# Decoder block with 32 experts on one core: the shared expert's gate and up products of later sequences at the end of the first stage, and later turns in an order written out

## The chip, the cores and the metric

The kernel runs on one core of one Trainium2 chip. The metric is the device time of one execution in microseconds (us), the median of three runs. PE is TensorE, DVE VectorE, ACT ScalarE, POOL GpSimd; SP only issues DMAs here.

## The reference

One post-norm decoder layer in float32 over 16 sequences of 256 tokens, width 256:

```
q, k, v = x Wq' + bq, x Wk' + bk, x Wv' + bv                # one head of 256
theta   = 0.5 + 0.2 sigmoid(qk) + 0.15 tanh(qk) + 0.1 relu(qk)
x1      = layernorm(x + softmax(theta) v Wo' + bo)
x2      = layernorm(x1 + cross attention(x1, ctx))          # 16 heads of 16, chunks of 64 tokens
scores  = sigmoid(x2 Wr')                                   # 32 experts in 4 groups
topk    = the 4 best experts out of the 2 best groups, weights normed to 2.5
mixed   = sum over the 4 of w * down_e( silu(gate_e x2) * up_e x2 )    # 128 inner
shared  = down_s( silu(gate_s x2) * up_s x2 )                          # 256 inner
out     = layernorm(x2 + mixed + shared)
```

## The kernel before

There are three stages. The first runs attention, cross attention, the router and the inner half of the shared expert, one sequence at a time in a software pipeline; each token's row is scattered to the region of each of its experts in `routed`. The second takes 159 blocks of 128 routed rows through their experts. The third adds the parts and normalizes.

The first stage is the subject. Every engine has its own instruction stream, in program order; semaphores join them. The order is written as a loop over turns `t` with one branch per step: turn `t` runs the first attention of sequence `t`, the cross attention of `t-2` and the router of `t-4`. After turn 15 the same loop runs six turns more, in which ever fewer steps are live; this text calls them the drain. A turn is counted from `pe_scores2(t-2)`, PE's scores of the cross attention (L398).

The steps that matter below:

- `pe_gate(i)` (L488) and `pe_up(i)` (L497): the shared expert's gate and up products, eight matmul records each, into PSUM banks 6 and 7. In the loop `pe_gate(t-4)` and `pe_up(t-5)` are in every turn. ACT makes tanh of the gate (`act_gates`, L841), DVE the two products (`vec_hs1`, L1065, and `vec_hs2`, L1070), and SP stores the result (`store_hs`, L1317) to `inner`, from where it is read in the second stage. `hs` has two buffers, so `act_gates(i)` waits for the store of `i-2`.
- `pe_scores1` (L338), then tanh on ACT (L761, L762), four instructions on DVE up to the row maximum `nmx` (`vec_th`, L943 to L949), exp on ACT (L768), and `pe_prT(t)` (L283 out of `pr_tile`): the softmax of the first attention leaves PE and comes back to it.
- `pool_xc` (L1239) and `pool_xc2` (L1256): residual sums on POOL, two instructions each. `pool_scattera` and `pool_scatterb` (L1263, L1269): four indirect DMAs each, 128 rows each.
- `pe_tables` (L512 to L522) with `vec_tables` (to L1120): the block tables, made once the last rank is known. SP's row loads of the second stage (L1370) wait for `v_adr` (L1119) and for every scatter.
- `load_rest` (L1328): the experts' weights, 768 KB for each sequence. The share of the first 14 comes during the turns. The room of the last two (`LATE = 2`) serves as work space in the first stage, so they are loaded only after the last `pe_scores2`.

## Time and profile before

| | us |
|---|---|
| median of three runs | 829.56 |
| the three runs | 825.52, 829.56, 829.70 |
| the profiled execution | 825.1 |
| its span, first to last instruction | 823.3 |
| PE busy, share of the span | 759.4, 92% |
| DVE busy | 581.7, 71% |
| ACT busy | 494.2, 60% |
| POOL busy | 367.9, 45% |

Busy time is what an engine's instructions took; matmul records overlap a little, so eight that the timeline lists with 1.89 us follow one another in 1.73 us, and the chain of waits shows the second number. A time below is in us from the span's start, if not said otherwise. What lies around the span is 1.8 us (825.1 less 823.3).

### The profile page before, as it was taken

What the parts mean: (1) busy time and instruction counts of PE and PEld (TensorE: products, weight loads), DVE (VectorE), ACT (ScalarE), POOL (GpSimd) and SP (SyncE); (2) the same over time, 40 slices, a digit from 0 to 9 for tenths busy, and PEclk for the clock granted to TensorE, in tenths of its full rate; (3) what the DMA queues carried; (4) which work ended last, traced back from release to release, by engine and by line L of the source; (5) the groups of instructions that cost most, each with busy time, mean ns of one, the idle gap of its engine ahead of it and who ended that gap; (6) DMA issues with size and microseconds to landing.
All of it is one profiled execution on the core that took longest, in us unless ns stands there. A gap on an engine that the chain in (4) does not pass through costs nothing.

```text
span 823.3 us, 21802 instructions
## 1 busy us (share of the span) xinstructions
PE 759.4 (92%) x8308; PEld 660.5 (80%) x8308; DVE 581.7 (71%) x2093; ACT 494.2 (60%) x1166; POOL 367.9 (45%) x437
## 2 busy tenths in 40 slices
PE   7969899999999999999987656799999999999996
PEld 6758788888888888888876536799999999998554
DVE  2345487898889888898898863466666666665585
ACT  0546666767777767767664414566666766663133
POOL 0110214335543455335545762466666666665142
PEclk9999999999999999999999977999999999999998
DMA  6572221332343334332113436755555555552996
GB/s 235 163 210 84 85 85 53 105 123 93 132 134 104 110 117 130 106 121 94 65 60 111 143 116 186 290 168 176 177 164 179 168 169 170 179 161 91 376 400 238
DMA packets 69642, 124.95 MB, mean 152 GB/s; under 512 B 9665, under 2 KB 43329, under 8 KB 69282
## 3 DMA queue, kind: packets, MB, share of 16 engines
q1 hardware_dynamic: 51394, 81.60, 31.4%
q0 software_dynamic: 13776, 37.77, 12.7%
q10 hardware_dynamic: 4368, 4.20, 1.5%
q8 instruction: 66, 1.08, 0.5%
q14 instruction: 38, 0.31, 0.1%
HBM read 73.16 MB, written 50.36 MB: 150 GB/s over the span
## 4 chain that ended last, share of the span: by engine, by line
PE 78%; DMA 7%; DVE 6%; SPq 5%; issue 2%; POOL 1%; ACT 1%; ACTq 0%; DVEq 0%
PE banks L537 17%; PE banks L283 10%; PE banks L544 8%; PE banks L385 4%; PE banks L376 3%; PE banks L353 3%; PE banks L321 3%; PE banks L366 3%; SPq L566 3%; PE banks L488 3%; PE banks L330 3%; PE banks L462 3%; PE banks L497 3%; PE banks L338 3%; DMA w_expert_tile<-y 2%; PE banks L428 2%
## 5 line engine op out<-in xcount | busy, mean ns | idle before, releaser
L1291 POOL DMA_INDIRECT y<-yb_tile,idcol_tile x159 | 152.4, 959 | 110.3 <-DVE yb_tile L1143 106.9
L537 PE MATMUL banks<-xbT_tile,wgu_tile 128*128 128x128 f32 x1272 | 170.4, 278 | 0.0
L537 PEld LDWEIGHTS banks<-xbT_tile,wgu_tile 128*128 128x128 f32 x1272 | 157.2, 195 | 0.1
L1143 DVE SCALAR_TENSOR_TENSOR yb_tile<-banks,rowsb_tile 128x256 f32<-128x256 f32 x159 | 76.9, 483 | 81.3 <-PE banks L544 73.1
L856 ACT ACTIVATE wgu_tile<-w_expert_tile 128x512 f32 x159 | 98.9, 622 | 11.8 <-DVE tab_i_tile L1120 11.8
L544 PE MATMUL banks<-w_expert_tile,hb_tile 128*128 x318 | 95.9, 384 | 4.8 <-DVE hb_tile L1131 4.8
L1269 POOL DMA_INDIRECT routed<-row_tile,idx_tile x64 | 62.5, 977 | 65.9 <-PE banks L398 50.4
L852 ACT ACTIVATE gb_tile<-banks 128x128 f32<-128x128 f32 x159 | 44.1, 277 | 77.5 <-PE banks L537 77.4
L1263 POOL DMA_INDIRECT routed<-row_tile,idx_tile x64 | 61.7, 963 | 30.7 <-issue 18.5
L1244 POOL TENSOR_TENSOR rs_tile<-ve_tile,half_neg_tile 128x2 f32<-128x2 f32 x16 | 11.1, 693 | 143.5 <-DVE ve_tile L959 143.5
L283 PE MATMUL banks<-const_tile,rowsb_tile 128*128 128x128 f32 x318 | 61.9, 277 | 7.1 <-DMA rowsb_tile<-routed 7.1
L723 ACT ACTIVATE xbT_tile<-banks 128x256 f32<-128x256 f32 x159 | 59.8, 376 | 12.2 <-PE banks L283 12.0
L283 PEld LDWEIGHTS banks<-const_tile,rowsb_tile 128*128 128x128 f32 x318 | 45.1, 143 | 23.5 <-DMA rowsb_tile<-routed 7.9
L544 PEld LDWEIGHTS banks<-w_expert_tile,hb_tile 128*128 128x128 f32 x318 | 48.5, 193 | 5.9 <-issue 5.9
L1131 DVE TENSOR_TENSOR hb_tile<-hb_tile,banks 128x128 f32<-128x128 f32 x159 | 45.8, 288 | 5.5
L1128 DVE SCALAR_TENSOR_TENSOR hb_tile<-gb_tile,banks 128x128 f32<-128x128 f32 x159 | 44.7, 281 | 3.9 <-ACT gb_tile L852 3.9
L1239 POOL TENSOR_TENSOR xc_tile<-x_sb_tile,c_out_tile 128x256 f32<-128x256 f32 x32 | 22.7, 734 | 54.7 <-ACT x_tile L815 27.7
L637 ACT ACTIVATE w_expert_tile<-w_expert_tile,fnmr_tile,frs_tile 128x256 f32<-128x256 f32 x32 | 17.6, 593 | 48.6 <-DVE fnmr_tile L617 48.6
L630 POOL TENSOR_TENSOR frs_tile<-fve_tile,fhalf_tile 128x2 f32<-128x2 f32 (+1 forms) x17 | 18.0, 1056 | 42.7 <-DVE fve_tile L612 42.7
L321 PE MATMUL banks<-xT_tile,g_qk_tile 128*128 128x256 f32 x128 | 32.4, 398 | 3.6 <-DMA xT_tile<-xT 3.6
L497 PE MATMUL banks<-x2T_tile,w_shared_in_tile 128*128 128x256 f32 x128 | 32.5, 400 | 1.3 <-ACT sc_tile L835 1.3
L594 PE MATMUL banks<-w_expert_tile,const_tile 128*128 128x512 f32 (+1 forms) x68 | 30.4, 580 | 3.5 <-DMA w_expert_tile<-y 3.5
(205 smaller groups left out, 1778.3 us busy)
## 6 DMA issues: line engine op xcount, KB each, us to landing
rowsb_tile<-routed SPq DMA_DIRECT2D x159, 129.0 KB, 2.2
w_expert_tile<-y SPq DMA_DIRECT2D x15, 1024.0 KB, 15.1
w_expert_tile<-w_expert SPq DMA_DIRECT2D x16, 768.0 KB
cT_tile<-ctxT SPq DMA_DIRECT2D x16, 384.0 KB, 2.9
routed<-zrow_tile SPq DMA_DIRECT2D x1, 4128.0 KB, 21.9
xT_tile<-xT SPq DMA_DIRECT2D x16, 256.0 KB, 3.1
x_sb_tile<-x SPq DMA_DIRECT2D x16, 256.0 KB, 2.8
inner<-hs_tile SPq DMA_DIRECT2D x16, 256.0 KB, 2.2
```

The lines of the kernel that those rows point to most:

```text
L283: return e.transpose(o, i, ident)
L321: m = e.matmul(bank[5][:, db * S:(db + 1) * S], g_qk[:, k, db * P:(db + 1) * P], xT[:, k, :], start=k == 0, stop=k == DK - 1)
L497: m = e.matmul(bank[7][:, b * S:(b + 1) * S], w_shared_in[:, k, 2 * P + b * P:3 * P + b * P], x2T[i % 2][:, k, :], start=k == 0, stop=k == ...
L537: m = e.matmul(bank[2 + u % 4][:, h * P:(h + 1) * P], wgu[u % WG][:, k * D + h * EI:k * D + (h + 1) * EI], xbT[u % 2][:, k * P:(k + 1) * P ...
L544: e.matmul(bank[6 + u % 2][:, 0:D], hb[u % 4][:, :], w_flat[:, bass.ds(w + 2 * D, D)], start=True, stop=True).then_inc(SEM["p_down"], 1)
L723: e.activation(o, i, ACT.Copy).then_inc(SEM[done], 1)
L856: e.activation(wgu[u % WG][:, :], w_flat[:, bass.ds(w, DK * D)], ACT.Copy)
L1131: e.tensor_tensor(hb[u % 4][:, :], hb1[u % 2][:, :], bank[2 + u % 4][:, EI:2 * EI], ALU.mult)\
L1143: e.scalar_tensor_tensor(yb[n % YS][:, :], bank[6 + u % 2][:, 0:D], rowsb[n % ROWS][:, D:D + 1], rowsb[n % ROWS][:, 0:D], ALU.mult, ALU.ad ...
L1263: e.indirect_dma_start(routed, bass.IndirectOffsetOnAxis(ap=idx[i % 2][:, 0, k:k + 1], axis=0), row[i % 2][:, k, 0, :], None).then_inc(SEM ...
L1269: e.indirect_dma_start(routed, bass.IndirectOffsetOnAxis(ap=idx[i % 2][:, 1, k:k + 1], axis=0), row[i % 2][:, k, 1, :], None).then_inc(SEM ...
L1291: e.indirect_dma_start(y, bass.IndirectOffsetOnAxis(ap=idcol[n % ROWS][:, :], axis=0), yb[n % YS][:, :], None).then_inc(SEM[f"st_y{n % YS} ...
```

## The change

Turns 0 to 7 stay in the loop. From the ninth on (turn 8) each engine has its own written list of steps, and the waits that belonged to the loop (`looped`) are written between the steps. Gate and up of sequences 4 to 15 are no longer in "their" turns: `pe_up(3)` is in turn 11, gate and up of 4 in turn 14, and the rest from turn 15 on. For this `x2T` has ten buffers instead of two. The room comes from the experts' weights: `qT`, `kM`, `vM`, `sha`, `shb` and both `prT` lie in it now, and `LATE` is 6, so the last six shares are loaded after the last `pe_av2`.

```diff
-        LATE = 3072 // SHARE
+        LATE = 9216 // SHARE
...
-        x2T = [sa(f"x2T{u}", [P, DK, S]) for u in range(2)]
+        x2T = [sa(f"x2T{u}", [P, DK, S]) for u in range(10)]
...
-        def pe_gate(e, i):
-            after(e, SEM["a_vo"], min(i + 5, nseq))
-            after(e, SEM["v_ve2"], min(i + 2, nseq))
+        def pe_gate(e, i, looped=True):
+            if looped:
+                after(e, SEM["a_vo"], min(i + 5, nseq))
...
-            for t in range(nseq + 6):
+            for t in range(8):
...
+            pe_out2(e, 14)
+            pe_x2T(e, 13, False)
+            e.wait_ge(SEM["v_ve2"], 15)
+            pe_gate(e, 7, False)
+            e.wait_ge(SEM["a_x2T"], 14)
+            pe_router(e, 13)
...
+            e.wait_ge(SEM["v_ve2"], 16)
+            pe_gate(e, 8, False)
+            e.wait_ge(SEM["a_sc"], 15)
+            pe_up(e, 8, False)
+            e.wait_ge(SEM["a_hg"], 9)
+            e.wait_ge(SEM["v_h1"], 9)
+            pe_gate(e, 9, False)
+            e.wait_ge(SEM["v_hs"], 9)
+            pe_up(e, 9, False)
...
         def act_gates(e, i):
             e.wait_ge(SEM["p_sg"], i + 1)
-            after(e, SEM["st_hs"], 16 * (i - 1))
+            after(e, SEM[f"st_hs{i % 2}"], 16 * (i // 2))
...
+            act_row(e, 14)
+            act_gates(e, 9)
+            act_norm2(e, 15)
+            act_x2T(e, 15)
...
+            vec_x2(e, 15, ch)
+            vec_route(e, 14, ch)
+            vec_hs1(e, 8, ch)
+            vec_hs2(e, 8, ch)
+            vec_choice(e, 14, ch)
+            vec_hs1(e, 9, ch)
+            vec_hs2(e, 9, ch)
+            vec_key(e, 14, ch)
+            vec_route(e, 15, ch)
...
                 if i == nseq - LATE:
                     e.wait_ge(SEM["p_s2"], nseq)
+                    e.wait_ge(SEM["p_av2"], nseq)
...
-                if live(t - 6):
+                if 0 <= t - 6 <= 2:
                     store_hs(e, t - 6)
+                if 3 <= t - 11 <= 3:
+                    store_hs(e, t - 11)
                 if 0 < t <= nseq - LATE:
                     load_rest(e, t - 1)
-                if nseq < t <= nseq + LATE:
-                    load_rest(e, t - 1 - LATE)
+            for i in range(4, 7):
+                store_hs(e, i)
+            for i in range(nseq - LATE, nseq):
+                load_rest(e, i)
+            for i in range(7, 16):
+                store_hs(e, i)
```

Three places show what moved. The first is PE in the middle of a turn, from the scores of the first attention to the transposes of its softmax. L338 (L341 after) is `pe_scores1`, L497 up, L488 gate, L376 (L382) `pe_v`, L366 (L371) `pe_k`; the L283 (L284) rows are transposes, those out of `pr_tile` being `pe_prT`. Before, in every turn:

```order
L338 MATMUL banks<-xT_tile,zT_tile 128x256 x4
L497 MATMUL banks<-x2T_tile,w_shared_in_tile 128x256 x4
L283 MATMUL banks<-const_tile,sha_tile 128x128 x8
L488 MATMUL banks<-x2T_tile,w_shared_in_tile 128x256 x4
L376 MATMUL banks<-w_cross_tile,cT_tile 128x128 x8
L283 MATMUL banks<-const_tile,x_tile 128x128 x4
L283 MATMUL banks<-const_tile,shb_tile 128x128 x8
L366 MATMUL banks<-cT_tile,w_cross_tile 128x256 x4
L283 MATMUL banks<-const_tile,pr_tile 128x128 x4
```

After, in turn 10 (L488 is the router there):

```order
L341 MATMUL banks<-xT_tile,zT_tile 128x256 x4
L488 MATMUL banks<-w_router_tile,x2T_tile 128x32 x4
L284 MATMUL banks<-const_tile,w_expert_tile 128x128 x8
L284 MATMUL banks<-const_tile,x_tile 128x128 x4
L382 MATMUL banks<-w_cross_tile,cT_tile 128x128 x8
L284 MATMUL banks<-const_tile,w_expert_tile 128x128 x8
L284 MATMUL banks<-const_tile,pr_tile 128x128 x4
L371 MATMUL banks<-cT_tile,w_cross_tile 128x256 x4
```

Gate and up are gone from between them, the router has come in from before `pe_scores1`, and `pe_k` stands behind `pe_prT`.

The second is PE's end of the first stage: the last products before the tables (L512 before, L520 after); L504 and L505 (L513, L514) are `pe_rank`, L479 (L488 after) the router. Before:

```order
L462 MATMUL banks<-w_cross_tile,num_tile 128x256 x4
L283 MATMUL banks<-const_tile,x_tile 128x128 x4
L479 MATMUL banks<-w_router_tile,x2T_tile 128x32 x4
L497 MATMUL banks<-x2T_tile,w_shared_in_tile 128x256 x4
L488 MATMUL banks<-x2T_tile,w_shared_in_tile 128x256 x4
...
L504 MATMUL banks<-msel_tile,const_tile 128x64
L505 MATMUL banks<-macc_tile,const_tile 128x64
L497 MATMUL banks<-x2T_tile,w_shared_in_tile 128x256 x4
L512 MATMUL banks<-const_tile,macc_tile 32x1
```

After (L497 is gate, L506 up), from the last router on:

```order
L488 MATMUL banks<-w_router_tile,x2T_tile 128x32 x4
L497 MATMUL banks<-x2T_tile,w_shared_in_tile 128x256 x4
L506 MATMUL banks<-x2T_tile,w_shared_in_tile 128x256 x4
L497 MATMUL banks<-x2T_tile,w_shared_in_tile 128x256 x4
L506 MATMUL banks<-x2T_tile,w_shared_in_tile 128x256 x4
L513 MATMUL banks<-msel_tile,const_tile 128x64
L514 MATMUL banks<-macc_tile,const_tile 128x64
L497 MATMUL banks<-x2T_tile,w_shared_in_tile 128x256 x4
L506 MATMUL banks<-x2T_tile,w_shared_in_tile 128x256 x4
L497 MATMUL banks<-x2T_tile,w_shared_in_tile 128x256 x4
L506 MATMUL banks<-x2T_tile,w_shared_in_tile 128x256 x8
L497 MATMUL banks<-x2T_tile,w_shared_in_tile 128x256 x8
```

Six pairs of gate and up (10 to 15) stand behind the last router, where one pair and one up stood, and two pairs (8 and 9) stand just before it.

The third is POOL in one turn, from its scatters on. L1239 (L1977 after) is `pool_xc`, L1256 (L1995) `pool_xc2`, L1250 (L1988) the power of the second norm. Before:

```order
L1269 DMA routed<-row_tile,idx_tile 135168x258 x4
L1263 DMA routed<-row_tile,idx_tile 135168x258 x4
L1239 TENSOR_TENSOR xc_tile<-x_sb_tile,c_out_tile 128x256 x2
L1256 TENSOR_TENSOR xc_tile<-x_tile,c_out_tile 128x256 x2
L1250 TENSOR_TENSOR rs_tile<-ve_tile,half_neg_tile 128x2
```

After, in turn 9:

```order
L2009 DMA routed<-row_tile,idx_tile 135168x258 x4
L2002 DMA routed<-row_tile,idx_tile 135168x258 x4
L1988 TENSOR_TENSOR rs_tile<-ve_tile,half_neg_tile 128x2
L1990 TENSOR_TENSOR nmr_tile<-neg_tile,rs_tile 128x2
L1977 TENSOR_TENSOR xc_tile<-x_sb_tile,c_out_tile 128x256 x2
L1995 TENSOR_TENSOR xc_tile<-x_tile,c_out_tile 128x256 x2
```

The power comes ahead of the sums in turns 8, 9, 11 and 13; in turns 10 and 12 `pool_xc` follows the scatters directly, as before.

## Rows read from the trace of the kernel before

**Rows 1.** Busy time in stretches: turns 8 to 15, the drain in two parts (columns: PE, PEld, DVE, ACT, POOL; clock)
```profile
208.00:420.40 212.40, 211.90 (x3074) 187.17 (x3072) 186.00 (x641) 151.89 (x330) 98.57 (x128) 1.00 0.32 108
420.40:459.50 39.10, 30.61 (x638) 25.64 (x638) 33.53 (x124) 20.67 (x32) 23.99 (x28) 1.00 0.28 98
459.50:498.20 38.70, 20.01 (x85) 14.72 (x83) 25.05 (x128) 8.04 (x11) 24.06 (x26) 0.78 0.37 129
```

**Rows 2.** Chain of waits in turn 13 (start, us, what)
```profile
340.75 1.14 PE banks L398 x63
...
344.20 0.81 PE banks L479 x8
...
348.56 1.73 PE banks L497 x8
...
357.71 0.43 PE banks L283 x4
```

**Rows 3.** Timeline of turn 13: the softmax outside PE, and POOL (start, us, engine)
```profile
342.18 1.04 POOL L1269 DMA_INDIRECT routed<-row_tile,idx_tile  x1 [4.35 <-PE banks L398]
...
348.60 0.47 ACT L761 ACTIVATE w_expert_tile<-banks,r_half_tile 128x256 f32<-128x256 f32 x1 [0.26 <-PE banks L338]
...
352.09 1.42 POOL L1239 TENSOR_TENSOR xc_tile<-x_sb_tile,c_out_tile 128x256 f32<-128x256 f32 x2
...
352.58 2.31 DVE L949 TENSOR_SCALAR nmx_tile<-mx_tile 128x2 f32<-128x2 f32 x1
...
353.46 1.40 POOL L1256 TENSOR_TENSOR xc_tile<-x_tile,c_out_tile 128x256 f32<-128x256 f32 x2
...
354.93 0.51 ACT L768 ACTIVATE pr_tile<-w_expert_tile,nmx_tile 128x256 f32<-128x256 f32 x1 [1.77 <-DVE nmx_tile L949]
```

**Rows 4.** Timeline: PE's first work of turns 8, 14, 16 and of the tables; DVE's addresses
```profile
208.16 1.21 PE L398 MATMUL banks<-kM_tile,qT_tile 32*64 32x128 f32 x64
...
367.19 1.21 PE L398 MATMUL banks<-kM_tile,qT_tile 32*64 32x128 f32 x64
...
420.41 1.21 PE L398 MATMUL banks<-kM_tile,qT_tile 32*64 32x128 f32 x64
...
486.22 0.20 PE L512 MATMUL banks<-const_tile,macc_tile 128*32 128x1 f32 x2 [1.34 <-DVE hs_tile L1070]
...
492.12 0.24 DVE L1119 TENSOR_SCALAR tab_i_tile<-tab_tile 1x160 int32<-1x160 f32 x1
```

**Rows 5.** Chain of waits at the end of the first stage
```profile
479.19 0.61 ACT hs_tile L841
...
494.63 2.56 DMA routed<-row_tile,idx_tile
497.28 0.72 SPq L269
498.21 0.36 SPq L1370
```

**Rows 6.** Busy time in three stretches: DVE from route to choice, its key and x2, one weight share
```profile
354.81:360.95 6.14, 6.14 (x95) 5.23 (x93) 5.52 (x39) 5.37 (x9) 0.96 (x3) 1.00 0.33 108
365.51:369.92 4.41, 4.41 (x82) 3.63 (x82) 4.10 (x18) 3.13 (x12) 1.04 (x1) 1.00 0.72 242
120.00:122.00 2.00, 2.00 (x68) 1.59 (x69) 1.07 (x4) 0.68 (x1) 0.00 (x0) 1.00 1.01 415
```

**Rows 7.** The page's DMA issues: count, KB each, median us to landing
```profile
routed<-zrow_tile SPq DMA_DIRECT2D x1, 4128.0 KB, 21.9
...
hs_sb_tile<-inner SPq DMA_DIRECT2D x1, 4096.0 KB, 14.5
```

**Rows 8.** Timeline of SP: the load of xT for turn 2
```profile
41.68 0.96 SPq L1301 DMA_DIRECT2D xT_tile<-xT  x1
```

**Rows 9.** Landing of a line's 16 DMAs: L1301 (loads of xT), then L1317 (stores of hs)
```profile
DMA to landing us min/median/max: 2.5/3.1/12.7
...
DMA to landing us min/median/max: 2.0/2.2/4.1
```

More of the change, by code:

```diff
@@ new lines, in _ @@
+            e.wait_ge(SEM["v_mxb"], 7)
+            e.wait_ge(SEM["v_shb"], 7)
+            pe_pTa(e, 6, False)
+            pe_x1T(e, 7)
+            e.wait_ge(SEM["a_vo"], 9)
+            pe_v(e, 8, False)
+            e.wait_ge(SEM["a_pTa"], 7)
+            pe_pTb(e, 6)
+            e.wait_ge(SEM["v_mx"], 9)
+            pe_prT(e, 8)
+            pe_k(e, 8)
+            e.wait_ge(SEM["a_pTb"], 7)
+            pe_av1(e, 8)
+            pe_den(e, 6)
+            pe_av2(e, 6, False)
+            pe_rank(e, 4)
@@ new lines, in _ @@
+            pe_scores1(e, 9)
+            e.wait_ge(SEM["a_x2T"], 6)
+            pe_router(e, 5)
+            e.wait_ge(SEM["v_mxa"], 8)
+            e.wait_ge(SEM["v_mxb"], 8)
+            e.wait_ge(SEM["v_shb"], 8)
+            pe_pTa(e, 7, False)
+            e.wait_ge(SEM["a_vo"], 10)
+            pe_v(e, 9, False)
+            pe_x1T(e, 8)
+            e.wait_ge(SEM["a_pTa"], 8)
+            pe_pTb(e, 7)
+            e.wait_ge(SEM["v_mx"], 10)
+            pe_prT(e, 9)
+            pe_k(e, 9)
@@ new lines, in _ @@
+            e.wait_ge(SEM["v_mxb"], 10)
+            e.wait_ge(SEM["v_shb"], 10)
+            pe_pTa(e, 9, False)
+            e.wait_ge(SEM["a_vo"], 12)
+            pe_v(e, 11, False)
+            pe_x1T(e, 10)
+            e.wait_ge(SEM["a_pTa"], 10)
+            pe_pTb(e, 9)
+            pe_k(e, 11)
+            e.wait_ge(SEM["v_hs"], 4)
+            pe_x2T(e, 8, False)
+            pe_prT(e, 11)
+            e.wait_ge(SEM["a_pTb"], 10)
+            pe_den(e, 9)
+            pe_av1(e, 11)
+            pe_av2(e, 9, False)
@@ new lines, in _ @@
+            pe_vo(e, 12, False)
+            e.wait_ge(SEM["a_z"], 13)
+            pe_scores1(e, 12)
+            pe_router(e, 8)
+            e.wait_ge(SEM["v_mxa"], 11)
+            e.wait_ge(SEM["v_mxb"], 11)
+            e.wait_ge(SEM["v_shb"], 11)
+            pe_pTa(e, 10, False)
+            pe_x1T(e, 11)
+            e.wait_ge(SEM["a_vo"], 13)
+            pe_v(e, 12, False)
+            e.wait_ge(SEM["a_pTa"], 11)
+            pe_pTb(e, 10)
+            e.wait_ge(SEM["v_mx"], 13)
+            pe_prT(e, 12)
@@ new lines, in _ @@
+            pe_scores1(e, 14)
+            e.wait_ge(SEM["a_vo"], 15)
+            pe_v(e, 14, False)
+            pe_gate(e, 4, False)
+            e.wait_ge(SEM["v_sha"], 13)
+            pe_pTa(e, 12, False)
+            pe_up(e, 4, False)
+            e.wait_ge(SEM["a_pTa"], 13)
+            pe_pTb(e, 12)
+            e.wait_ge(SEM["v_mx"], 15)
+            pe_prT(e, 14)
+            pe_k(e, 14)
+            e.wait_ge(SEM["a_pTb"], 13)
+            pe_den(e, 12)
+            pe_av1(e, 14)
+            e.wait_ge(SEM["v_h1"], 5)
@@ L860, in _ @@
             e.wait_ge(SEM["v_setup"], 1)
-            for t in range(nseq + 6):
+            for t in range(8):
                 if live(t - 4):
@@ L1275, in _ @@
             e.wait_ge(SEM["v_setup"], 3)
-            for t in range(nseq + 6):
+            for t in range(8):
                 if live(t - 6):
```

797 lines of the change are left out of this document (748 added, 49 removed).

## The prediction

> **What bounds the kernel now.** I read the page's slices first: PE is nine tenths busy nearly everywhere, with one dip in the middle, at the end of the first stage. Busy time in stretches gives it numbers [rows 1]: in turns 8 to 15 PE is busy 211.9 of 212.4 us, so PE sets the pace there and every PE instruction costs its full time. In the first half of the drain it is busy 30.6 of 39.1 us, in the second 20.0 of 38.7, and there the granted clock is 0.78: part of it ran at 1.2 GHz instead of 2.4, after gaps of PE. So 27 us of PE lie idle in the drain, while gate and up, which nothing needs before the second stage, stand in the full turns. Then the chain of waits: in a turn it is all PE [rows 2]; at the end of the first stage it runs from the last sequence's router over DVE to POOL's eight scatters, whose last lands at 497.2, and SP starts the row loads 0.93 us later, at 498.2 [rows 5]. The addresses for them are ready at 492.4 [rows 4], so the tables are not what ends the stage; the scatters are.
>
> **The turns (8 to 13).** Six turns take (367.19 - 208.16) / 6 = 26.51 us each [rows 4]. Gate and up are 1.73 us each [rows 2], so PE's own work in a turn falls to 26.51 - 3.46 = 23.05. Whether the turn gets there is decided by what the two products covered: the way of the softmax out of PE and back. In before, PE leaves `pe_scores1` at 348.56 and starts `pe_prT` at 357.71, 9.15 us later, all filled [rows 2]. In after, router, `pe_pTa`, `pe_x1T`, `pe_v` and `pe_pTb` stand between: 9.15 less gate and up (3.46) less `pe_k` (1.73, eight records of the same size as up) plus the router's 0.81, 4.8 us. The way itself: tanh starts at 348.60 and `nmx` at 352.58, 3.98 [rows 3]; `nmx` alone is some 0.2 when nothing stops it; two exps of 0.51 and handing over 1.1; with hops 5.4. So the turn becomes one chain: PE from `pe_scores2` to the end of `pe_scores1` without the router, 348.56 - 340.75 - 0.81 = 7.0; the softmax 5.4; and from `pe_prT` to the next turn 367.19 - 357.71 = 9.48, plus `pe_k` 1.73, 11.2. That is 23.6; I add 0.2, since DVE now waits once for `pe_vo`: 23.8. On DVE the turn is 186.0 / 8 = 23.3 busy [rows 1], less 1.2 for the two products that go with gate and up, 22.1 at most: close behind, not ahead.
>
> `nmx` is the weak place. It took 2.31 us and ended at 354.89, just as POOL's four sums did (353.46 + 1.40 = 354.86) [rows 3]: a tiny DVE instruction held up while POOL adds in SBUF. In before that was hidden by the 9.15. In after, `nmx` starts 7.0 + 4.0 = 11.0 us into the turn, and POOL's sums could start 352.09 - 340.75 = 11.3 us in, where they follow the scatters directly (turns 10 and 12), and 1.0 later where the power stands ahead. So it slips through by 0.3 us in two turns and by 1.3 in four. I price turns 10 and 12 at 2.0 together (bounds: nothing, and 2 x 2.8). Turn 11 carries `pe_up(3)`, 1.73, of which a little fills a gap: 1.4. Sum 6 x 23.8 + 2.0 + 1.4 = 146.2 against 159.0: -12.8. Bounds: at PE's own work -19.0, at the old turn length 0.
>
> **Turns 14 and 15.** Turn 14 has gate and up as before: 26.6. Turn 15 has gate but no up, and `pe_v(15)` and `pe_out2(13)` (1.78 each, as eight such records) go over to turn 16: 26.5 - 1.7 - 3.6 = 21.2 of PE, with waits 22.6. Together 49.2 against 420.41 - 367.19 = 53.2: -4.0.
>
> **The drain.** Up to `pe_out2(15)` before takes 39.1 [rows 1]. After, I walked through the written lists step by step with the durations of the trace: turn 16 holds 18.9 us of PE and takes 20, turn 17 holds 14.8, but waits for DVE's four passes over banks 0 to 3 and takes 20: 40.0 in all, +0.9. The fillers (up 5, gate and up 6, gate and up 7) are free there.
>
> Behind it stand eight pairs of gate and up, 27.7 us, and 3.7 of transposes, routers and ranks: 31.4 of PE. DVE has route and choice twice (6.14 less one product, 5.5 each), key and x2 4.4, key twice more 5.0, and sixteen products of 0.6: 30 [rows 6]. Two engines with 31 and 30 that hand each other every bank do not overlap fully. Step by step from the end of `pe_out2(15)`: gate 8 waits for x2 (2.7), gate 9 for the product of 8, which stands behind route 14 (7.2), gate 10 at 13.4, gate 11 behind route 15 (18.4), gate 13 behind key 15 (25.9), then 3.6 us per pair (gate 1.73, ACT 0.61 [rows 5], product 0.6, hops), the last up ends at 38.5, the tables start at 39.4. Before, it was 486.22 - 459.5 = 26.7: +12.7. Bounds: 31.4 without a wait, +4.7; PE with the two routes and the last key laid bare, 31.4 + 11 + 2.5, +18.2. I take the walk, near their middle.
>
> **The store behind the weights.** SP now issues six weight shares (4.72 MB) after the last `pe_av2`, and `store_hs(7)` behind them; `act_gates(9)` waits for that store, and gate 10 and the second norm of 15 for ACT. A store lands in 2.2 us as a rule [rows 9]. But the load issued at 41.68 [rows 8] came behind the 4128 KB that landed in 21.9 us [rows 7], and is the one of 12.7 among 16 loads with a median of 3.1 [rows 9]. At the rate of a weight share, 415 GB/s [rows 6], the six take 11.4 us; at that of the `hs_sb` load, 4096 KB in 14.5 us [rows 7], 16.3. Gate 9 ends 12.6 us after `pe_av2(15)`; with 0.6 for issue and 2.2 for landing the store is 1.6 or 6.5 us late. Bounds 0 (no order between them) and 6.5; I take +2.5, near the row of the same kind of transfer. The weights themselves are in some 30 us before they are needed.
>
> The Trainium skill, "DMA: Bandwidth & Descriptors", section "Queues, rings and completion order", says that each DMA engine consumes the descriptors of one ring in ring order, SP having one ring on each. By that rule the store waits for all six shares and the term is 1.6 to 6.5; with shares moved side by side it would be 0. The load of 12.7 us above agrees with the rule.
>
> **The end of the stage.** The last key now ends 25 us after `pe_out2(15)`, the scatters are through 13 us later and landed before the tables are done. SP is released by the addresses: 492.36 + 0.93 = 493.3 in before's terms, not 498.2: -4.9. The short matmuls of the tables still leave PE idle before the second stage, so I leave its first blocks at the lower clock as they are.
>
> **Sum.** -12.8 - 4.0 + 0.9 + 12.7 + 2.5 - 4.9 = -5.6 us on the profiled execution's 825.1: 819.5. The median shown is 829.56, 4.5 above that execution (the three runs are 825.5, 829.6, 829.7); the same step from it gives 824.0. I forecast between the two: 822.
>
> **Rivals.**
> - *PE's own work is reached.* The softmax fits (5.4 against 4.8 is a close call), no stop in turns 10 and 12, and the store is free: 6 x 23.05 + 1.7 = 140.0 instead of 146.2, and 2.5 less: 810.8. For it: PE had not one gap in these turns. Against: the chain counted above.
> - *DVE takes the turn over at 25.* POOL's sums then hold up not `nmx` but a copy in `vec_route` (up to 1.4 us for one pair), and `vec_rden`, `vec_x1`, `vec_o` come late for `pe_spread` and `pe_out2`. 6 x 1.2 more: about 826 to 827, no change.
> - *Slower: `nmx` is stopped in every turn.* If it starts after POOL's first sum, it waits until POOL's pairs are over, 2.8 us, now uncovered: the turn is 23.6 + 2.8 = 26.4 again. In all six, 14.8 more than I count: 834.3. It is slower than before as soon as about four turns more than counted are stopped. For it: a margin of 0.3 us in two turns, and it happened in turn 13. Against: 1.3 us in the other four.
> - That gate and up stay where they were is excluded by the order of PE.
>
> **How the numbers follow.** A measurement here can tell about 0.5%, 4.1 us, from no change. The forecast (815 to 824 on the profiled scale) 0.46, of which 0.33 is faster by more than that; PE's own work 0.17, faster; turns of 25 us 0.22, same 0.17; stopped every turn 0.15, slower 0.13. Faster 0.53, same 0.32, slower 0.15. The range 811 to 831 goes from the first rival to the stopped turns in part; the likeliest case alone is 815 to 828, the difference between runs included.
>
> **What would show it.** `pe_scores2` to `pe_scores2` in turns 8 to 13: 23.8; a gap of PE before `pe_prT` under 1 us; `nmx` at 0.2 us, and at 1.5 or more where stopped. Turn 16 starts at 403.6, the tables at 485.5, the first row load at 492.6 with no wait for a scatter. ACT's `act_gates(9)` released by a DMA, not by PE. It is wrong if turns stay above 25, if the stage's tail is longer than 43 us from `pe_out2(15)`, or if SP still waits for scatters.

## The result, and the profile after

The changed kernel took 837.13 us (median of five runs, 833.12 to 839.35) against 827.09 for before (five runs): ratio 1.0097, interval 1.0067 to 1.0127. Forecast was 822 with a range of 811 to 831, so the sign was wrong as well as the size. The profiled execution took 835.56 us, its span 833.7. In three of the five sessions below every kernel, before included, took 4 to 5% longer (before at 860 to 871 us, elsewhere at 827 to 830), so a ratio is always to before in the same session.

The stages, from the starts of the same matmuls in the two traces (before [rows 4, 5]; "forecast" are the terms of the prediction; the last row counts from the end of `pe_out2(15)`, as the row above it does):

| stretch, us | before | forecast | after |
|---|---|---|---|
| start of turn 8 | 208.16 | 208.2 | 209.85 |
| turns 8 to 13 | 159.0 | 146.2 | 149.5 |
| turns 14, 15 | 53.2 | 49.2 | 48.8 |
| turn 16 to the end of `pe_out2(15)` | 39.1 | 40.0 | 43.0 |
| from there to the tables | 26.7 | 41.9 | 49.6 |
| from there to the first row load | 38.7 | 49.0 | 56.7 |

The misses are +3.3, -0.4, +3.0, +7.7, and +1.7 for the start, 15.3 of the 16.1 by which the execution is over the 819.5 of the sum. The start stays open: six later runs of the new order began turn 8 at 206.8 to 209.7, one of them, the unchanged kernel again, at 209.65. The same stretches as busy time (stretch; then per engine us busy and instructions; granted clock of PE, DMA share, GB/s), where [rows 1] has those of before:

```profile
209.85:359.34 149.49, 142.19 (x2217) 125.79 (x2216) 128.88 (x473) 108.36 (x235) 75.31 (x96) 0.99 0.29 97
359.34:408.10 48.76, 47.58 (x733) 41.55 (x733) 41.97 (x151) 38.23 (x83) 24.66 (x32) 1.00 0.22 70
408.10:451.10 43.00, 35.51 (x670) 31.11 (x671) 36.34 (x134) 21.06 (x35) 24.02 (x28) 1.00 0.27 94
451.10:500.70 49.60, 37.14 (x160) 30.54 (x158) 27.66 (x119) 10.99 (x16) 24.02 (x26) 0.86 0.49 187
451.10:507.80 56.70, 40.23 (x172) 31.88 (x170) 31.20 (x135) 10.99 (x16) 24.02 (x26) 0.83 0.44 168
467.00:480.00 13.00, 10.23 (x33) 8.52 (x34) 8.64 (x44) 4.67 (x7) 6.27 (x7) 0.56 0.22 80
```

First column after the length: PE. Up to the first row load it idles 7.3 + 1.2 + 7.5 + 16.5 = 32.5 us; in before it was 0.5 + 8.5 + 18.7 = 27.7 [rows 1]. The change moved PE's idle time and made it 4.8 us longer. 12.5 us of it lie between `pe_out2(15)` and the tables, and there a stretch of 13 us ran at a clock of 0.56. The waits around 467 us (start, us, engine line; in brackets idle time before, and who ended it) say why:

```profile
446.93 4.29 SPq L2133 DMA_DIRECT2D w_expert_tile<-w_expert  x6
451.26 0.44 SPq L2121 DMA_DIRECT2D inner<-hs_tile  x1
466.88 0.60 ACT L1233 ACTIVATE hs_tile<-banks 128x512 f32<-128x512 f32 x1 [9.02 <-DMA inner<-hs_tile]
467.50 0.69 DVE L1650 SCALAR_TENSOR_TENSOR hs_tile<-hs_tile,banks 128x512 f32<-128x512 f32 x1 [6.74 <-ACT hs_tile L1233]
469.04 1.11 PE L284 MATMUL banks<-const_tile,x_tile 128*128 128x128 f32 x4 [6.51 <-DVE hs_tile L1656]
470.88 1.89 PE L488 MATMUL banks<-w_router_tile,x2T_tile 128*128 128x32 f32 x8 [0.73 <-ACT x2T_tile L1111]
472.58 3.76 PE L497 MATMUL banks<-x2T_tile,w_shared_in_tile 128*128 128x256 f32 x8
476.14 3.04 PE L506 MATMUL banks<-x2T_tile,w_shared_in_tile 128*128 128x256 f32 x8
```

SP issues the six weight shares, then the store of `hs(7)`; it lands 15.5 us later. ACT's gate 9 waits for it, DVE's products for ACT, and PE's transposes of `x2(15)` for DVE. Behind the gap PE runs at 1.2 GHz: a gate takes 3.76 us where it took 1.97 to 2.00 in front. And who lets SP start the row loads:

```profile
SPq L270 <- DVE tab_i_tile L1702: 5.6, 1, 5.6
507.80 1.41 SPq L2181 DMA_DIRECT2D rowsb_tile<-routed  x3
```

The addresses, as forecast, and no scatter any more (before: [rows 5]).

### The profile page after: what moved, and what is told of

It reads as the page before. It is cut to its first block, busy times and chain, and to the rows that moved or that the text cites. A ratio compares the mean times of both kernels' runs of the same rounds, so it can differ in the third digit from the quotient of the medians.

```text
span 833.7 us, 21846 instructions
## 1 busy us (share of the span) xinstructions
PE 763.7 (92%) x8308; PEld 664.2 (80%) x8308; DVE 575.1 (69%) x2093; ACT 493.3 (59%) x1166; POOL 369.5 (44%) x437
## 4 chain that ended last, share of the span: by engine, by line
PE 75%; DMA 8%; DVE 8%; SPq 5%; issue 2%; ACT 1%; POOL 0%; ACTq 0%; DVEq 0%
PE banks L545 17%; PE banks L284 9%; PE banks L552 8%; PE banks L390 4%; PE banks L323 3%; PE banks L470 3%; PE banks L497 3%; PE banks L506 3%; PE banks L382 3%; PE banks L333 3%; PE banks L371 3%; PE banks L356 3%; SPq L574 3%; DMA w_expert_tile<-y 2%; PE banks L404 2%
## 5 line engine op out<-in xcount | busy, mean ns | idle before, releaser
L2002 POOL DMA_INDIRECT routed<-row_tile,idx_tile x64 | 62.7, 980 | 41.2 <-PE banks L404 23.0
L284 PE MATMUL banks<-const_tile,rowsb_tile 128*128 128x128 f32 x318 | 62.1, 278 | 2.1 <-DMA rowsb_tile<-routed 2.1
L284 PEld LDWEIGHTS banks<-const_tile,rowsb_tile 128*128 128x128 f32 x318 | 45.3, 143 | 18.5 <-DMA rowsb_tile<-routed 2.8
L1977 POOL TENSOR_TENSOR xc_tile<-x_sb_tile,c_out_tile 128x256 f32<-128x256 f32 x32 | 22.8, 734 | 55.8 <-ACT x_tile L1208 28.5
L284 PE MATMUL banks<-const_tile,w_expert_tile 128*128 128x128 f32 x256 | 33.6, 274 | 9.2 <-DVE w_expert_tile L1575 8.5
L284 PEld LDWEIGHTS banks<-const_tile,w_expert_tile 128*128 128x128 f32 x256 | 28.7, 141 | 12.1 <-issue 10.1
L497 PE MATMUL banks<-x2T_tile,w_shared_in_tile 128*128 128x256 f32 x128 | 32.7, 401 | 4.6 <-DVE hs_tile L1650 2.8
```

Source lines behind the costliest of these rows:

```text
L284: return e.transpose(o, i, ident)
L497: m = e.matmul(bank[6][:, b * S:(b + 1) * S], w_shared_in[:, k, 0 * P + b * P:1 * P + b * P], x2T[i % 10][:, k, :], start=k == 0, stop=k = ...
L2002: e.indirect_dma_start(routed, bass.IndirectOffsetOnAxis(ap=idx[i % 2][:, 0, k:k + 1], axis=0), row[i % 2][:, k, 0, :], None).then_inc(SEM ...
```

## The experiments

Only the sessions in which before took 827 to 830 us decide here; the runs of the others have a section of their own below. An indented paragraph is what was expected, as it was written before the run.

**1. The store first.**

```
-            for i in range(4, 7):
+            for i in range(4, 8):
                 store_hs(e, i)
             for i in range(nseq - LATE, nseq):
                 load_rest(e, i)
-            for i in range(7, 16):
+            for i in range(8, 16):
```

> The changed kernel with the store of hs(7) ahead of the six weight shares, once more, since in its first run the chip took 4% longer for the kernel before as well: some signals of PE in the middle of a turn came up to 4 us after the matmul there (p_pTa 3.2 us, in the first traces 0.3). If this chip delivers them in 0.3 us as the first one did, the theory of the store gives a tail from the end of out2(15) to the tables of 40 to 42 us instead of 49.7, no gap over 1.5 us before x2T(15) or its router, and 7 to 9 us less than the changed kernel in all (ratio to before 0.998 to 1.002). If the signals are late again, the gap of 3.5 us before router(15) comes back and the gain is 2 to 4 us as in the first run.

Measured: 828.27 us, ratio 1.001 (0.9982 to 1.0037); the unchanged `after_3` beside it 836.34, 1.0126 (1.0072 to 1.0181). From the end of `pe_out2(15)` to the tables 41.2 us against 48.7. The landing (issue form, KB, us to landing) of `hs(7)`, and PE's rows that answer to those above:

```profile
inner<-hs_tile SPq DMA_DIRECT2D x1, 256.0 KB, 2.9
```
```profile
467.02 0.66 PE L284 MATMUL banks<-const_tile,x_tile 128*128 128x128 f32 x4 [0.39 <-DVE hs_tile L1656]
468.41 1.05 PE L488 MATMUL banks<-w_router_tile,x2T_tile 128*128 128x32 f32 x8 [0.73 <-ACT x2T_tile L1111]
469.29 3.20 PE L497 MATMUL banks<-x2T_tile,w_shared_in_tile 128*128 128x256 f32 x8
472.29 2.39 PE L506 MATMUL banks<-x2T_tile,w_shared_in_tile 128*128 128x256 f32 x8
```

The gap is 0.39 us where `after_3` has 5.88, and the router runs at full speed (1.05 us; the gate behind it still takes 3.20). So the place of the store costs 7.5 us in the tail and 8.1 in the whole: 5.5 as a gap, and the other 2.0 where PE ran at the lower clock behind it. The rest of the tail, 41.2, is my walk of 39.4 and 1.8.

> The changed kernel, unedited, beside the three. Timely signals: turns 9 to 13 of 23.5 to 25.5 and ratio 1.007 to 1.013, tail 49 to 50 us with a gap of 6 to 7 us before x2T(15). Late signals: turns of 26 to 29 and ratio 1.013 to 1.02.

`after_3` repeats the first execution: turns 8 to 13 149.9, the tail 48.7.

**2. Three shares ahead, and the shares in another queue.**

```
-            for i in range(nseq - LATE, nseq):
-                load_rest(e, i)
-            for i in range(7, 16):
+            for i in range(nseq - LATE, nseq - LATE + 3):
+                load_rest(e, i)
+            store_hs(e, 7)
+            for i in range(nseq - LATE + 3, nseq):
+                load_rest(e, i)
+            for i in range(8, 16):
```

> The changed kernel with three of the six shares ahead of the store of hs(7) and three behind it. Theory of order: the store lands about 1 us behind the third share, 8 to 10 us after the last av2 (with all six ahead 15.5 us after its issue, with none ahead 2.9 us), so at 457 to 460 where gate 9 ends at 460.3: gate 9 waits under 1 us, the tail from out2(15) to the tables is 41 to 42 us as with the store first, ratio 0.999 to 1.003. Theory of bandwidth (transfers share the engines whatever their order): it lands nearly as late as with six ahead, 13 us or more after its issue, and gate 9 waits 5 us.

826.62 us, ratio 0.9961 (0.9932 to 0.9991). The third share, and the store issued right behind it:

```profile
w_expert_tile<-w_expert SPq DMA_DIRECT2D x1, 768.0 KB, 9.5
inner<-hs_tile SPq DMA_DIRECT2D x1, 256.0 KB, 9.8
```

Landing after 2.9, 9.8 and 15.5 us with none, three and six shares ahead: in one queue it is the bytes ahead that count. At 9.8 gate 9 is not held up (tail 41.2 again). The ratio is a little below the 0.999 to 1.003 expected.

```
             act_num(e, 15)
+            e.wait_ge(SEM["p_s2"], nseq)
+            e.wait_ge(SEM["p_av2"], nseq)
+            for i in range(nseq - LATE, nseq):
+                e.dma_start(w_flat[...], d["w_expert"]...)   # on ACT; taken out of SP's list
```

> The changed kernel with the six late weight shares issued by ACT, not SP; in its first run signals of PE came late and landings were recorded in part. Here the store of hs(8), issued about 8 us behind the shares, moves while they do. Theory of order: it lands 2 to 4 us after its issue (with the store first and the shares in SP's own queue it took 7.5 us, from 463.2 to 470.7, just behind the last share), that of hs(7) under 4 us, and the whole is 7 to 10 us under the changed kernel (ratio 0.999 to 1.003 on a chip with timely signals). Theory of bandwidth: the store of hs(8) lands only 6 to 8 us after its issue, when the shares are through, in this queue too.

828.11 us, ratio 0.9988 (0.996 to 1.0017), tail 41.2. But the theory of order fails here. The stores of `hs(7)`, issued together with ACT's first share, and of `hs(8)`, issued at 456.4 with the last shares still moving:

```profile
inner<-hs_tile SPq DMA_DIRECT2D x1, 256.0 KB, 5.9
```
```profile
inner<-hs_tile SPq DMA_DIRECT2D x1, 256.0 KB, 7.0
```

A queue to itself did not free `hs(8)`: 7.0 us, and 7.5 in the run with the store first, where it stood behind the shares in SP's queue. It landed at 463.4, and the last share, issued at 448.0, after 15.2 us at 463.2. Even `hs(7)`, with no share ahead of it, doubled from 2.9 to 5.9, where the first share took 6.0. So what is in flight in the other queue counts too. `hs(7)` was both early and in a queue of its own here; which of the two brought it from 15.5 to 5.9 is not separated.

**3. The eight pairs left out.** `after_less_2` and `before_less_2` are the two kernels without gate and up of sequences 8 to 15, their activations and their products (the stores of these sequences store the buffer of sequence 7).

```
-            pe_gate(e, 8, False)
-            pe_up(e, 8, False)
...
-            vec_hs1(e, 15, ch)
-            vec_hs2(e, 15, ch)
```

> The kernel before without gate and up of sequences 8 to 15, once more. Timely signals: turns without the two are 23.0 to 24.0 us and the whole 14 to 20 us under before (ratio 0.976 to 0.983), because PE sets the turn there. Late signals: turns of 27.5 to 29, ratio 1.00 to 1.01, because the turn is then a chain through ACT that the two products had covered.

829.87 us, ratio 1.0018 (0.999 to 1.0047): 27.7 us of PE's work taken out, and none of the gain of 14 to 20 us that I expected. Busy time of before in turns 13 to 15, then of this kernel in the same turns, in the drain up to `pe_out2(15)`, and from there to the row loads:

```profile
340.70:420.40 79.70, 79.52 (x1153) 70.21 (x1152) 69.67 (x241) 56.36 (x122) 36.97 (x48) 1.00 0.27 91
```
```profile
343.10:421.30 78.20, 71.80 (x1109) 60.61 (x1109) 66.36 (x235) 54.99 (x121) 36.96 (x48) 1.00 0.30 99
421.30:467.70 46.40, 30.95 (x607) 27.10 (x607) 32.58 (x124) 19.55 (x29) 24.00 (x28) 0.71 0.33 115
467.70:503.40 35.70, 9.66 (x44) 6.83 (x42) 21.54 (x120) 7.07 (x9) 24.04 (x26) 0.55 0.25 90
```

Three turns lose about 10 us of gate and up and get 1.5 us shorter. The drain gets 7.3 us longer than the 39.1 of before, at a granted clock of 0.71 where it was 1.00 [rows 1]. In the old order the pairs cost nothing in sum: in turns 13 to 15 PE is now idle for 6.4 us, and in the drain, with fewer products, it is as long busy as before (30.95 us against 30.6), since much of that time is at its lower level. From `pe_out2(15)` to the row loads this kernel takes 35.7 us, before 38.7.

> The changed kernel without gate and up of sequences 8 to 15, on a chip with timely signals if it is one. Theory (the written order is worth its 9.5 us in turns 8 to 13 whether or not the pairs come later, and the end without them is bound by routes and keys on DVE): out2(15) ends at 450 to 453 as in the changed kernel, the tables start 25 to 29 us later, ratio 0.975 to 0.985; then the pairs at the end cost 22 us or more of their 27.7, though PE idles 27 us in the old drain. Rival (the order's gain in the turns rests on the deferral alone and is lost again at the end by the same chain): the tables start 35 us or more after out2(15), ratio 0.99 or more. With late signals: turns of 27 to 30 and ratio 1.01 or more, which tells nothing of this.

821.76 us, ratio 0.9911 (0.9872 to 0.9949), the profiled execution 813.67. Turns 8 to 13 take 148.2, and the tables start 25.3 us after `pe_out2(15)`, as the theory had it; the gain is less than its 0.975 to 0.985, since the tables do not set the end. The end, from `pe_out2(15)` to the row loads, what released SP, and POOL's first scatter of this stretch, its one wait, and its last:

```profile
447.90:485.90 38.00, 9.59 (x45) 6.87 (x42) 21.54 (x120) 6.96 (x9) 24.03 (x26) 0.57 0.67 252
```
```profile
SPq L2123 <- DMA routed<-row_tile,idx_tile: 26.7, 1, 26.7
```
```profile
450.29 0.72 POOL L1938 TENSOR_TENSOR rs_tile<-ve_tile,half_neg_tile 128x2 f32<-128x2 f32 x1 [5.80 <-DVE ve_tile L1505]
451.81 1.04 POOL L1952 DMA_INDIRECT routed<-row_tile,idx_tile  x1 [0.53 <-issue]
473.47 0.96 POOL L1959 DMA_INDIRECT routed<-row_tile,idx_tile  x1 [1.64 <-DVE row_tile L1645]
482.32 0.96 POOL L1952 DMA_INDIRECT routed<-row_tile,idx_tile  x1 [0.30 <-issue]
```

Without a single pair the end still takes 38.0 us, as before's 38.7 with its own, and again a scatter ends it. What fills it is POOL: from 451.8 on it issues the 24 scatters of sequences 13, 14 and 15, one every 1.26 us, and waits for DVE only once in between (1.64 us). That is a floor: 30.5 us from the first to the last, 2.4 to its landing, 1.2 to the row loads. It starts 3.9 us after `pe_out2(15)`, since in the written list POOL's power of sequence 15, which waits 5.8 us for DVE, stands ahead of the scatters of 13; in `before_less_2` the first of the last 24 starts after 0.7 us, and its end takes 35.7. Of PE's time only 9.6 of 38.0 us are in use, so eight pairs (27.7) have just room under the floor. In the changed kernel they cost 56.7 - 38.0 = 18.7 us there, 9.5 of them (47.5 - 38.0) also with the store first.

**4. The tables between the pairs.** If the floor is what counts, nothing on it, and not the tables either, may stand behind a pair. The tables need the last key, not the pairs 12 to 15:

```
             pe_gate(e, 12, False)
             e.wait_ge(SEM["v_hs"], 12)
             pe_up(e, 12, False)
+            pe_tab1(e)              # waits for v_key of 16; banks 2 to 5, not 5 to 7
...
             pe_gate(e, 13, False)
+            pe_tab2(e)
...
             pe_up(e, 13, False)
+            pe_tab3(e)
...
             pe_gate(e, 15, False)
+            pe_tab4(e)
...
-            pe_tables(e)
```

DVE's steps go the same way; `hs` has four buffers, SP issues the store of `hs(7)` ahead of the weights, and those of 12 to 15 behind the first eight row loads.

> The changed kernel with the tables between pairs 12 to 15, four buffers of hs and the store first, once more on another chip if it is one. On a chip with timely signals: turns of 23.5 to 25, row loads at 40 to 44 us behind out2(15) (56.7 in the changed kernel), 12 to 17 us under the changed kernel, ratio to before 0.985 to 0.995. On one with late signals: turns of 27 to 29 and a ratio of 1.01 to 1.02, as in its first run.

819.08 us, ratio 0.9887 (0.9825 to 0.9948): faster than both, 17 us under `after_3` and 9.2 under the run with the store first. What of these 9.2 is the tables' place, and what the four buffers and the later stores, was not separated. SP's wait and the row loads:

```profile
SPq L2190 <- DMA routed<-row_tile,idx_tile: 13.7, 1, 13.7
```
```profile
491.25 3.99 SPq L2198 DMA_DIRECT2D rowsb_tile<-routed  x8
```
```profile
452.30:494.80 42.50, 37.27 (x178) 29.78 (x175) 31.36 (x137) 12.09 (x19) 24.29 (x26) 0.96 0.59 220
```

The row loads start 38.9 us after `pe_out2(15)`, released by a scatter again: the floor is reached with all eight pairs under it, at 0.9 us more than with none. POOL issues its 24 scatters from 456.2 to 488.6 here, with waits for DVE of 0.5 and 2.0 us. PE is busy for 37.3 of the 42.5 us up to the first block, at a clock of 0.96.

**5. PE's stop in turn 8.** In every run of the new order up to here PE stops in turn 8 with 59 of the 64 matmuls of `pe_spread` done, for 2.0 to 4.6 us, with no wait behind it that the profile shows, and for 0.7 to 2.1 us more in turn 9, with four of the eight matmuls of `pe_q` done. In before there is none. Turns 8 to 13 took 148.2 to 154.8 us in these seven runs. The changed kernel, and `tables_early_2`:

```profile
231.75 0.31 PE L462 MATMUL banks<-rden_tile,const_tile 128*32 128x64 f32 x5 [2.16 <-issue]
```
```profile
230.79 0.31 PE L462 MATMUL banks<-rden_tile,const_tile 128*32 128x64 f32 x5 [4.17 <-issue]
```

To `tables_early_2` I added 96 PE instructions in front, which do nothing new:

```
+            for again in range(25):
                 for k in range(DK):
                     e.matmul(bank[2][:, 0:1], rep[:, k, 0, :], b_attn[:, k, 1:2], start=k == 0, stop=k == DK - 1)
```

> The kernel with the tables between the pairs, with 48 more matmuls of one column in PE's setup (96 PE instructions more; they repeat a result). It shifts every later instruction of PE by 96 places. Theory (PE's stop in turn 8, 2.2 to 4.9 us at its instruction 5567 each time, and the one in turn 9 at 6337, come from the supply of instructions, in blocks of 256, so their place is one in memory): the stops move by one in the program, to another group of matmuls 96 instructions earlier, or vanish where the code there is slower to run. Rival (they come from the code of turn 8 itself): the stop stays before the same matmuls of the spread, with 59 of 64 done. The price of the added matmuls is 1 to 4 us before turn 1.

833.91 us, ratio 1.0063 (1.0032 to 1.0095): the added matmuls moved turn 8 from 206.9 to 227.9, far more than I had said. But the stops are gone. `pe_spread` of turn 8, and turns 8 and 9 together, then 8 to 13, of this kernel; below them turns 8 and 9 of `tables_early_2`:

```profile
246.61 1.10 PE L463 MATMUL banks<-rden_tile,const_tile 128*32 128x64 f32 x64
```
```profile
227.90:275.20 47.30, 45.63 (x733) 40.57 (x732) 42.89 (x158) 36.12 (x79) 26.54 (x34) 1.00 0.37 128
227.90:372.30 144.40, 140.14 (x2223) 124.32 (x2222) 128.81 (x472) 108.32 (x235) 75.55 (x96) 1.00 0.30 100
```
```profile
206.90:262.50 55.60, 47.82 (x737) 41.94 (x736) 42.52 (x159) 36.20 (x80) 26.30 (x34) 0.97 0.33 109
```

So the stop belongs to the place of the instructions, not to what they do. In both orders one instruction block of 16 KB arrives in this stretch (a queue of the kind "instruction", 1 packet of 0.02 MB from 229 to 232 us), in before without a stop. That PE waits for it in the new order is my reading and not shown. The Trainium skill, "Runtime: NRT & Kernel Launch", section "Instruction fetch mechanics", says that blocks of 16 KiB, 256 instructions, are fetched ahead and that this is hidden by the time that instructions take. The size agrees with the packet. If the stop is a wait for instructions, it speaks against the second, in a stretch where 64 matmuls and their 64 weight loads pass in 1.1 us; no run here shows that it is.

The same shift by smaller matmuls, in the changed kernel and in the one with early tables, beside which before took 861 us:

> The changed kernel with 48 added small matmuls (32 columns of weights, one moving column, 96 PE instructions, a result that is written over) in PE's setup, some 1 to 2 us in all. Theory (the stops of 2.2 us before the spread in turn 8 and 1.4 us before q in turn 9, with their slower matmuls behind them, come from the supply of instructions at fixed places in memory): turns 8 and 9 together 47.0 to 48.0 us instead of 52.5, and the whole 2 to 5 us under the changed kernel, ratio to before 1.003 to 1.010. Rival (they come from the code of the turn, and the earlier shift hid them only because the long start changed the timing): both stops are back at the same matmuls, ratio 1.010 to 1.015.

> The kernel with the tables between the pairs, four buffers of hs and the store first, with the same 48 small matmuls in the setup. Theory: turns 8 and 9 together 47.0 to 48.0 us instead of 55.6 as it had without, the rest as there, so 811 to 816 us, ratio to before 0.980 to 0.986. Rival: the stops are back, ratio 0.986 to 0.992 as without the shift.

873.6 us, ratio 1.0162 (1.0102 to 1.0222), and 868.65, 1.0141 (1.0075 to 1.0208). The stop inside `pe_spread` in turn 8 is gone in both traces (in the six unshifted kernels of the new order where before took 860 or 871 us it is there, 1.3 to 1.7 us each). In the second, turn 8 starts at 211.1, within 1.3 us of its unshifted kernel, so it is not the 21 us of later start that took the stop away. In both, other waits decide the time, and both ratios miss what I expected. What the stop is worth in the whole time stays open; 149.5 - 144.4 = 5.1 us in turns 8 to 13 is what the traces give, of which 2.9 are the two stops of the changed kernel and most of the rest the slower matmuls behind the first.

## The runs beside which before took 860 to 871 us

Ten runs fell into sessions in which the kernel before took 860, 871 and 861 us (the last two runs above are two of them); on one chip before took 871 us in one session and 827 in another, so it is no property of a chip. Four tell something.

> The kernel before, unedited, for its profile beside the other three on the same chip. If this chip is like the first, its turns are 26.4 us with PE never idle and the whole 825 to 830 us; if it is like the one of the four runs before (before at 860 us), its profile shows where PE is idle there: then ACT's copy of the first four transposes (pTa) starts 2 to 4 us late with no visible releaser in the old order too.

> The changed kernel again, unedited, beside the three others on the same chip. If the 1.7 us by which its turn 8 starts later (209.85 against 208.16) and the stop of PE of 2.2 us in turn 8 are its own, they come back in this profile within 0.5 us; if they are chance of one execution, one of them is gone. The time against the kernel before is 1.007 to 1.013.

> The changed kernel with one edit: SP issues the store of hs(7) ahead of the six weight shares instead of behind them. Theory (the store stood behind 4.72 MB in SP's queue, PE idled 6.5 us behind it and then ran 13 us at a granted clock of 0.56): the store lands about 2.5 us after hs(7) is through, the activation of gate 9 is released by PE, the gap of 6.51 us before x2T(15) goes down to 1 us or less, the granted clock of the stretch behind it stays near 1, and the tail from the end of out2(15) to the tables is 37 to 41 us instead of 49.7; the whole falls by 9 to 13 us against the changed kernel, to 824 to 828. The store of hs(8) still stands behind the shares and may hold gate 10 for 1 to 2 us. Rival (the tail is set by the chain of routes and keys on DVE and the gap only covered it): the gap moves to another place, the tail stays above 46 us, the time falls by under 3 us.

> The changed kernel with three edits: the matmuls and DVE steps of the tables are put between the pairs 12 to 15 (in other banks) right behind the last key instead of behind the last pair; hs has four buffers and the stores of 12 to 15 go behind the first eight row loads; the store of hs(7) goes ahead of the weights. Theory (what ends the stage is the list: the tables wait behind pairs that they do not need, and PE then idles for 7 us until the first rows are there): the row loads are issued 12 to 17 us earlier, about 40 us after the end of out2(15) instead of 56.7, the pairs fill PE's idle time, and the whole is 12 to 17 us shorter than the changed kernel, 4 to 8 us shorter than before (ratio 0.990 to 0.995). Rival (scatters and the store chain end last in any order): the row loads wait for a scatter at 50 us or more, and the kernel is no faster than before.

Measured: `before_again` ratio 1.000 (0.9968 to 1.0032) at 870.13 us, `after_again` 1.016 (1.011 to 1.0211), `a_store_first` 1.0113 (1.0065 to 1.0162), `g_tables_early` 1.0177 (1.0143 to 1.0211). In the session at 871 us `before_again` took 164.9 us for turns 8 to 13 and the new order (`g_tables_early`) 171.3: it lost 6.4 where it had gained 9.5. In that at 860 us the new order took 158.1 us (`a_store_first`) to 165.5 (`after_again`), and there is no trace of before beside them. What PE waits for is seen in `after_again`:

```profile
329.04 1.95 PE L382 MATMUL banks<-w_cross_tile,cT_tile 128*128 128x128 f32 x16
332.94 1.02 ACT L1193 ACTIVATE w_expert_tile<-banks 128x1024 f32<-128x1024 f32 x1 [3.60 <-remote]
334.02 1.97 PE L284 MATMUL banks<-const_tile,w_expert_tile 128*128 128x128 f32 x8 [3.03 <-ACT w_expert_tile L1193]
```

ACT copies the transposes that PE records before 329.04, but starts 3.6 us after its last work, released, by the profile, by something "remote" and not by PE; PE then waits for ACT. In the first profile of the changed kernel ACT never waits at that line in turns 8 to 13. In `before_again` ACT's copy comes late by the same 3.6 us in four of the turns (L801), but there gate and up cover it: PE is busy for 160.2 of 164.9 us, in `after_again` for 146.7 of 165.5. Why the signals come late there stays open. Of the expectations, those of the store and of the tables failed: with the store first the tail was 46.7 us, and with the early tables the row loads came 44.4 us after `pe_out2(15)`.

The first runs of four other kernels:

> The changed kernel with one edit: ACT issues the six late weight shares, behind the copy of num(15), instead of SP; the store of hs(7) stays on SP in its place. Theory of order (stores wait for what was put into the same queue before them): the store of hs(7) lands within 5 us of its issue although the same 4.72 MB are moving at the same time, and gate 9 waits under 1 us for it; the issues cost ACT some 4.3 us in an idle stretch of 4.1 us before x2T(14), so up to 1 us is lost there; the whole falls by 8 to 12 us against the changed kernel. Theory of bandwidth (4.72 MB in flight slow any transfer): the store again takes 10 to 15 us, gate 9 waits 6 us or more, the time stays within 3 us of the changed kernel's.

> The changed kernel with one edit: hs has four buffers instead of two, so gate 9 waits for the store of hs(5), which is long through, and gate 11 for that of hs(7). The order of the queue is left: the store of hs(7) still lands some 15 us after its issue. Theory (the cost comes from that wait and from the clock behind it): gate 9 is released by PE, gate 11, some 8 us later than gate 10, waits at most 1 us, the clock stays near 1 in the tail, and the whole falls by 9 to 13 us against the changed kernel, as with the store first. Rival (the moving weights themselves slow PE, ACT or DVE, or the clock falls for another reason): the clock is again near 0.6 behind gate 10 and the time falls by under 4 us.

> The kernel before without the gate and up products of sequences 8 to 15 and what follows from them (their activations and the two products on DVE; the stores of these sequences store the buffer of sequence 7 instead). Its own order is left. What it is for: beside the same cut in the changed kernel it splits the price of these eight pairs by place. Theory A (the pairs cost PE's full time in turns 12 to 15, and some in the drain, where PE waits anyway): the whole is 14 to 20 us shorter than before, a turn with neither product is 23.0 to 24.0 us, the drain gives the rest. Theory B (the pairs covered the softmax also in the old order, whose turn then hits the chain through ACT and DVE): a turn stays at 25 us or more and the whole is under 12 us shorter.

> The changed kernel without the same eight pairs (gate and up of sequences 8 to 15, their activations, their products; stores as in the other cut kernel), so without all of the PE work that it keeps for the end but the last ranks, x2T and routers. Theory A (the keeping is what costs: eight pairs at the end take more there than they gave back in the turns): this kernel is 20 us or more faster than the changed one (the tail from the end of out2(15) to the tables about 27 us, as before the change), and 5 to 12 us faster than before. Theory B (the written order itself is worse): it is no faster than the cut kernel in the old order, and under 15 us faster than the changed one. With 27.7 us of PE work left out, the difference to 27.7 is what the pairs add or save beyond their own length.

Ratios 1.0086 (1.005 to 1.0121), 1.0171 (1.0126 to 1.0217), 1.0039 (1.001 to 1.0068) and 1.0142 (1.0093 to 1.0192). Four buffers of `hs` gave nothing there: the tail was 46.1 us, with the store first 46.7, unchanged 47.8, since a gap of 3.5 us before router 15 came in the place of the one before x2T(15). No gain that I had expected of these four came, and they decide nothing for the sessions at 827 to 830 us. Whether four buffers alone would do there what the store first did was not run.

## Why the prediction was wrong

- **The turns (forecast -12.8, measured -9.5).** The chain was counted right: turns 10 to 13 took 23.8, 25.4, 23.6 and 24.3 us, and without the stops all six take 144.4. `nmx` took 0.17 us in each of the six, where before it had 2.31 [rows 3]: in turns 10 and 12 POOL's first sum started 1.4 us after it, where I had counted 0.3, so the two stops that I priced at 2.0 did not come, nor did the rival that stops it in every turn. What I left out is PE's own stop in turns 8 and 9, 5.1 us. Nothing in before's rows of these turns shows it; it comes with the place of the code. In `store_first_2` it took most: turns 8 to 13 were 154.8 us there, 10.4 more than without the stops.
- **Turns 14 and 15 (-4.0, measured -4.4).** Right.
- **The drain to `pe_out2(15)` (+0.9, measured +3.9, and +4.7 to +5.8 in the runs of Experiments 1 to 5 at 827 to 830 us).** Two waits of PE for DVE in turn 17, before gate 7 and `pe_pTa(15)` (1.7 and 2.2 us), are there in all of these that have the pairs; my walk had DVE earlier.
- **The tail (+12.7, measured +14.5 with the store out of the way).** The walk of 39.4 holds within 1.8.
- **The store behind the weights: the step that failed most.** I gave it +2.5, from the one share that moved at 415 GB/s [rows 6], with the bounds 0 and 6.5. It measured 7.5 in the tail. The late landing was near my upper bound, worked out from the 14.5 us of the 4096 KB load [rows 7]: the six shares and the store took 19.9 us from the first issue, 5.0 MB or 250 GB/s, slower than either row (POOL's scatters moved beside them, 329 GB/s in all), and gate 9's activation came 6.5 us late, as in my upper bound. And I priced the wait alone; behind a gap of 6.5 us PE ran 13 us at a clock of 0.56, 2 us more. I had the row with the landing of 12.7 us behind a large transfer [rows 9], which pointed to the upper end, and took 2.5.
- **The end of the stage (-4.9).** Right as a mechanism and wrong as a gain: the addresses release SP 7.1 us after the tables, as forecast, but only because they come so late. Against the floor of 38 us, which POOL's scatters set, there was nothing to win.
- **The sum.** The deeper fault is in the first paragraph of the prediction: "27 us of PE lie idle in the drain, while gate and up, which nothing needs before the second stage, stand in the full turns". The idle time was real, but the end of the stage has a length of its own: POOL's 24 scatters behind the keys, 35.7 to 38.0 us to the row loads even without the pairs. The written list put the keys and tables that lead there behind the pairs: the routers, ranks and tables stand in PE's order behind pairs that they do not need. And "every PE instruction costs its full time" in turns 8 to 15 did not hold for the old order: with some 10 us of gate and up left out of turns 13 to 15, these became 1.5 us shorter, and the drain 7.3 longer. In the new order the turns did fall to some 24 us; how much of that is the pairs' leaving and how much the rest of the written list was not separated. I had no rival in which the list at the end, with its store, costs more than the turns give.

## What to carry to other kernels

Before work is moved into an engine's idle stretch, find the chain that sets that stretch's length, and put no link of it behind the fillers in the engine's list: the same eight pairs cost 9.5 us with the tables behind them and the store out of the way (18.7 with the store behind the weights), and 0.9 with the tables between them, four buffers and later stores. A store that frees a buffer goes ahead of bulk loads; price it at the slowest row of such a load, and add the lower clock behind the gap. And leaving work out is a test of what it costs: eight pairs that filled 27.7 us of PE were worth nothing where they stood.

## What the runs showed of the chip that I had not expected

- A 256 KB store took 2.9 us issued just ahead of six shares of 768 KB, 9.8 and 15.5 us behind three and six of them in one queue, and 5.9 and 7.0 us from a queue of its own while shares moved in another (7.5 when issued 8 us behind them in the same queue).
- PE stops for 1.3 to 4.6 us at one fixed instruction in all 13 unshifted runs of the new order, and 96 instructions put in front take the stop away in three of three.
- POOL issued one scatter of 128 rows every 1.26 us, and 24 of them in a row set the length of the stage's end.
- With less work for PE the drain got longer: 46.4 us at a granted clock of 0.71 against 39.1.
